# Layer 0: the tap path for three groups in four, indicator rows at image edges alone, the output's sum on GpSimd, and a new order of the work

## The reference

```
h  = w_hidden (384 x 64) * groupnorm(x) + b_hidden
h  = depthwise 3x3 convolution of h (w_dw, zero padding) + b_dw
q, k, v = h in three parts of 128 channels
out = irfft2(rfft2(q) * rfft2(k))      on patches of 8 x 8 pixels
out = layernorm of out over its 128 channels, times ln_w, plus ln_b
x   = x + w_proj (64 x 128) * (v * out) + b_proj
```

## Time and profile before

| | us |
|---|---|
| median of 3 runs | 8750.6 |
| lowest and highest | 8746.06 and 8751.87 |
| the profiled execution | 8754.59 |
| its span, first to last instruction | 8752.8 |

### The profile page before, as it was taken

How to read it: one execution, slowest core, us unless ns; L and a number is a source line. 1 busy time by engine, 2 the same in 40 slices (tenths; PEclk the granted TensorE clock), 3 DMA queues, 4 the chain that set the end, 5 groups by cost and what they waited for, 6 DMA issues and landing times. The chain is left out here.

```text
span 8752.8 us, 169999 instructions
## 1 busy us (share of the span) xinstructions
PE 8435.8 (96%) x57716; PEld 4818.6 (55%) x57716; DVE 7480.2 (85%) x9839; ACT 6324.6 (72%) x8629; POOL 4840.4 (55%) x2723
## 2 busy tenths in 40 slices
PE   2999999999999999999999999999879999999999
PEld 1666666666666666666666666666323333333333
DVE  6888888888888888888888888888759999999998
ACT  2777777777777777777777777777208888888887
POOL 1444444444444444444444444444109999999998
PEclk9999999999999999999999999999999999999999
DMA  6222222222222222222222212212694555555554
GB/s 154 54 68 61 55 68 63 55 67 54 64 68 53 64 56 66 64 56 65 64 49 55 54 43 54 54 43 54 146 203 114 119 119 119 119 119 119 119 119 111
DMA packets 613650, 711.27 MB, mean 81 GB/s; under 512 B 44029, under 2 KB 572507, under 8 KB 589575
## 3 DMA queue, kind: packets, MB, share of 16 engines
q1 hardware_dynamic: 611022, 690.44, 33.9%
q10 hardware_dynamic: 2488, 18.98, 1.0%
HBM read 548.96 MB, written 164.11 MB: 81 GB/s over the span
## 5 line engine op out<-in xcount | busy, mean ns | idle before, releaser
L625 PE MATMUL banks<-w_hi,hi_lo 128*128 128x256 f16 x18432 | 2362.6, 273 | 35.1 <-DVE hi_lo L927 35.1
L625 PEld LDWEIGHTS banks<-w_hi,hi_lo 128*128 128x128 f16 x18432 | 1737.7, 98 | 844.9 <-issue 533.5
L583 POOL TENSOR_TENSOR u_im<-q_im,k_swap 128x512 f32<-128x512 f32 x512 | 741.3, 1448 | 1810.4 <-ACT q_im L821 1723.8
L959 DVE SCALAR_TENSOR_TENSOR v_s<-banks,tap_w,v_s 128x512 f32<-128x512 f32 x2048 | 1535.1, 750 | 55.0 <-ACT v_s L810 0.6
L1511 PE MATMUL banks<-z,conv_w 128*128 128x512 f32 x3096 | 1556.0, 618 | 1.2 <-ACT z L1639 1.2
L1482 POOL TENSOR_TENSOR part_sum<-part_sum,prod 128x1024 f32<-128x1024 f32 x645 | 1525.2, 2365 | 52.2
L795 ACT ACTIVATE qk<-banks,inv_wscale 128x512 f32<-128x512 f32 x1024 | 706.5, 690 | 910.2 <-PE banks L625 903.7
L586 POOL TENSOR_TENSOR u<-u,u_im 128x512 f32<-128x512 f32 x512 | 725.3, 1417 | 766.8 <-DVE u L936 766.8
L625 PE MATMUL banks<-w_lo_pair,hi_pair 128*128 128x256 f16 x6144 | 1006.1, 273 | 0.0
L592 POOL TENSOR_TENSOR u<-u,u_mean 128x512 f32<-128x512 f32 x512 | 532.2, 1040 | 733.7 <-DVE u_mean L967 733.7
L1511 PEld LDWEIGHTS banks<-z,conv_w 128*128 128x128 f32 x3096 | 521.5, 188 | 628.1 <-issue 570.5
(11 more groups left out here) (252 smaller groups left out, 15777.1 us busy)
## 6 DMA issues: line engine op xcount, KB each, us to landing
xr<-in_x_dram SPq DMA_DIRECT2D x258, 640.0 KB, 9.1
xb<-y_scratch SPq DMA_DIRECT2D x262, 320.0 KB, 4.7
xa<-y_scratch SPq DMA_DIRECT2D x262, 256.0 KB, 5.4
x_res<-in_x_dram SPq DMA_DIRECT2D x258, 256.0 KB, 4.1
out_dram<-res SPq DMA_DIRECT2D x258, 256.0 KB, 3.3
y_scratch<-ys SPq DMA_DIRECT2D x256, 256.0 KB, 3.9
prod<-y_scratch SPq DMA_DIRECT2D x256, 256.0 KB, 5.6
xs<-in_x_dram SPq DMA_DIRECT2D x92, 512.0 KB, 7.4
```

The source lines that it names most:

```text
L583: nc.gpsimd.tensor_tensor(u_im[:], q_im[:], k_swap[:], ALU.mult).then_inc(u_made, 1)
L625: r = pe.matmul(out, px, w, start=n == 0, stop=n == 13)
L959: v.scalar_tensor_tensor(v_out, hidden_v[:, 1 + dc:GCOL + 1 + dc, 1 + dr:R + 1 + dr], tap_w[:, t:t + 1], v_out, ALU.mult, ALU.add).then_in ...
```

## The change

1. In each strip group 0 takes v from `conv_v`, groups 1, 2 and 3 from `hidden` and taps (before: 0 and 2, and 1 and 3). Every tap round is again one instruction on ScalarE and eight on VectorE.
2. The indicator rows L910 are written only where the strip's number is known when built and it, or the strip two before it, lies at an image's edge.
3. The sum `ys + t_n` is an instruction of GpSimd (`output_sum`), with new semaphores `t_made` and `fin_step`; VectorE keeps its statistics.
4. `means` becomes `sums` and `means`, `finish` becomes `scaled` and `shifted`, `imaginary` becomes `imaginary` and `complex_sum`, `root` and `freq_copy` are split likewise. All engines have a new order, written for one strip (`for h in range(2)`), and deeper: `body` is also issued for -1, 64 and 65, with filters `real...` for what does not exist. Every `forward` stands right behind another block and its wait is put ahead of that block's last matmul (`then_forward`). GpSimd does both halves of the low parts in a row. `hi_stacks` signals `tops_ready` of its own. The strip's statistics of x are read a body later.

The core of the diff (j = 4h, jp = 2h, js = h; lines marked with - are those of before, on the same engine):

```diff
# GpSimd
                 def body(i, first, stats, image, last):
-                    for k in range(8):
-                        if k % 4 == 2:
-                            pool.wait_ge(u_ready, i * 8 + (k - 1))
-                            low_parts(i * 2 + (k // 4 + 1), 0)
-                        if not (first and k == 0):
-                            imaginary(i, k, not (first and k == 1))
-                            less_mean(i, k)
-                        if k % 4 == 2:
-                            pool.wait_ge(u_ready, i * 8 + k)
-                            low_parts(i * 2 + (k // 4 + 1), 1)
+                        imaginary(i, j)
+                        complex_sum(i, j)
...
+                        low_parts(i, js + 1, 0)
+                        low_parts(i, js + 1, 1)
+                        less_mean(i, j)
+                        imaginary(i, j + 1)
+                        complex_sum(i, j + 1)
+                        less_mean(i, j + 1)
+                        imaginary(i, j + 2)
+                        complex_sum(i, j + 2)
+                        output_sum(i, jp - 1)
+                        less_mean(i, j + 2)
+                        imaginary(i, j + 3)
+                        complex_sum(i, j + 3)
+                        less_mean(i, j + 3)
+                        output_sum(i, jp)
+                def output_sum(i, jp):
+                    if real_pair(i, jp):
+                        out = ys[jp // 2 % 2][:, :, GCOL * (jp % 2):GCOL * (jp % 2) + GCOL]
+                        pool.wait_ge(fin_read, i * 4 + (jp + 1))
+                        pool.wait_ge(t_made, i * 4 + (jp + 1))
+                        nc.gpsimd.tensor_tensor(out, out, t_n[:].rearrange("p (c r) -> p r c", r=R), ALU.add).then_inc(fin_step, 1)
# TensorE
+                        inverse(i, j - 2)
+                        project(i, jp - 2, j - 1)
+                        value(i, j, image if h == 0 else None, then_forward=j)
+                        forward(i, j)
+                        hidden(i, j + 1, jp - 2)
+                        tile(i, j + 1, 0)
+                        tile(i, j + 1, 1)
+                        inverse(i, j - 1)
+                        tile(i, j + 1, 2)
+                        tile(i, j + 1, 3)
+                        variance(i, jp - 1)
+                        tile(i, j + 2, 0)
+                        project(i, jp - 1, j + 1, then_forward=j + 1)
+                        forward(i, j + 1)
+                        tile(i, j + 2, 1)
+                        hidden(i, j + 2, jp - 1)
+                        tile(i, j + 2, 2)
+                        inverse(i, j)
+                        tile(i, j + 2, 3)
+                        tile(i, j + 3, 0)
+                        tile(i, j + 3, 1, then_forward=j + 2)
+                        forward(i, j + 2)
+                        tile(i, j + 3, 2)
+                        tile(i, j + 3, 3)
+                        hidden(i, j + 3, jp - 1)
+                        inverse(i, j + 1)
+                        tile(i, j + 4, 0)
+                        tile(i, j + 4, 1)
+                        variance(i, jp, then_forward=j + 3)
+                        forward(i, j + 3)
+                        tile(i, j + 4, 2)
+                        tile(i, j + 4, 3)
# ScalarE
+                        qk_copy(i, j, 1)
+                        high_parts(i, js + 1)
...
+                        v_copy(i, j)
+                        first_tap(i, j + 1)
+                        query_imaginary(i, j)
+                        key_swap(i, j)
+                        square(i, j - 1)
+                        query_real(i, j)
+                        qk_copy(i, j + 1, 0)
+                        log_root(i, jp - 1)
+                        exp_root(i, jp - 1)
+                        qk_copy(i, j + 1, 1)
+                        query_imaginary(i, j + 1)
+                        qk_copy(i, j + 2, 0)
+                        first_tap(i, j + 2)
+                        query_real(i, j + 1)
+                        key_swap(i, j + 1)
+                        square(i, j)
...
# VectorE
+                        for row, col, edge in ((0, 4, 0), (R - 1, 5, S - 1)):
+                            if isinstance(s, int) and (s < 2 or s % S == edge or (s - 2) % S == edge):
+                                v.tensor_scalar(hi_ind[b][C:P, 1:W + 1, row], ind[C:P, :, row], par[b][C:P, col:col + 1], None, ALU.mult)
+                    if image is not None:
+                        x_chunk(i)
+                        next_means(image)
+                    for h in range(2):
+                        j, jp, js = 4 * h, 2 * h, h
+                        taps(i, j - 1, 2, 3)
+                        times_v(i, j - 3)
+                        taps(i, j - 1, 3, 4)
+                        sums(i, j - 2)
+                        taps(i, j - 1, 4, 5)
+                        means(i, j - 2)
+                        taps(i, j - 1, 5, 8)
+                        masks(i, js + 1)
+                        product(i, j - 1)
...
+                        shifted(i, jp - 2)
+                        scaled(i, jp - 2)
+                        output(i, jp - 3)
+                        if h == 0 and stats and not first and image is None:
+                            x_chunk(i)
+                        sums(i, j - 1)
...
+                        times_v(i, j - 2)
+                        means(i, j - 1)
+                        taps(i, j + 1, 0, 6)
+                        product(i, j)
+                        taps(i, j + 1, 6, 7)
+                        times_v(i, j - 1)
+                        taps(i, j + 1, 7, 8)
+                        output(i, jp - 2)
+                        sums(i, j)
+                        high_below(i, js + 1)
+                        means(i, j)
+                        scaled(i, jp - 1)
+                        high_stacks(i, js + 1)
+                        taps(i, j + 2, 0, 1)
+                        params(i, js + 2)
+                        taps(i, j + 2, 1, 3)
+                        product(i, j + 1)
+                        taps(i, j + 2, 3, 5)
+                        times_v(i, j)
+                        taps(i, j + 2, 5, 6)
+                        sums(i, j + 1)
+                        taps(i, j + 2, 6, 7)
+                        means(i, j + 1)
+                        taps(i, j + 2, 7, 8)
+                        both_stacks(i, js + 1)
+                        taps(i, j + 3, 0, 1)
+                        shifted(i, jp - 1)
+                        taps(i, j + 3, 1, 2)
+                        product(i, j + 2)
```

More of the change, by code:

```diff
@@ L527, in body @@
                     for b in range(2):
[L528 removed]
+                        if not last:
                             of, halves_before = i * 2 * R + (b + 2) * R, i * 4 + 2 * b + 2
@@ new lines, in inverse @@
+                def inverse(i, j, then_forward=None):
+                    if real(i, j):
+                        pe.wait_ge(u_ready, i * 8 + (j + 1))
+                        need(pe, w_ready, i * 8 + j)
+                        by_patch = b_o[:].rearrange("c (half t p x) -> c p t half x", half=2, t=2, p=2)
+                        for p in range(2):
+                            for t in range(2):
+                                block = slice(P * (2 * p + t), P * (2 * p + t) + P)
+                                if p and t and then_forward is not None:
+                                    transform_ready(i, then_forward)
+                                last = pe.matmul(by_patch[:, p, t], u[:, block], idft[:], start=True, stop=True)
+                        last.then_inc(inv_done, 1)
+                    elif then_forward is not None:
+                        transform_ready(i, then_forward)
@@ new lines, in variance @@
+                def variance(i, jp, then_forward=None):
+                    if real_pair(i, jp):
+                        pe.wait_ge(sq_ready, i * 8 + (2 * jp + 2))
+                        need(pe, fin_read, i * 4 + jp)
+                        for h in range(2):
+                            if h and then_forward is not None:
+                                transform_ready(i, then_forward)
+                            last = pe.matmul(b_var[C * h:C * h + C, :], mean_w[:, 0:C], sq[h][:], start=True, stop=True)
+                        last.then_inc(var_done, 1)
+                    elif then_forward is not None:
+                        transform_ready(i, then_forward)
@@ L761, in tail @@
-                def tail():
-                    transform_ready(NB, -1, True)
-                    forward()
-                    inverse(NB, -1, True)
-                    project(NB, 0)
-                    inverse(NB, 0, True)
-                    variance(NB, 1, True)
-                    project(NB, 2)
-                run(pe, body, tail)
+                    for h in range(2):
+                        j, jp, js = 4 * h, 2 * h, h
+                        inverse(i, j - 2)
```

(1 more changed line is left out.)

654 lines of the change are left out of this document (315 added, 339 removed).

## The result

The changed kernel takes 8945.5 us (median of 4 runs, 8943.4 to 8954.9) against 8748.3 of the kernel before (8745.6 to 8751.9): ratio 1.0226, interval [1.0214, 1.0239]. It is slower by 197 us; 8586 was predicted, and 8700 was the upper end. The profiled execution took 8943.63 us, with a span of 8941.8.

What follows compares the result with a forecast made beforehand. TensorE's instruction stream was taken as the bound, 46.8 us a strip. Strips of 45.3 give -192, x statistics +12, image edges +16: -164 from 8754.6, less 4 for the median, 8586 us; range 8410 to 8700.

Steps and rivals of the forecast that it cites:

- the chain by hand: Hand-traced sequence of one strip across the engines, with GpSimd holding VectorE: 45.3 us a strip in place of 46.8; chance 0.55.
- The first stack copy near 2.7 in place of 0.83: VectorE's first stack copy, held beside GpSimd's low part, was to take near 2.7 us in place of 0.83.
- Second low part 2.7: 22.3: GpSimd's second low part takes 2.7 us and ends 22.3 us after the strip's start in the hand-traced sequence.
- The sum of the output: Two sums a strip leave VectorE for GpSimd: 2 x 1.09 us and a wait, 2.4 us off VectorE.
- The indicator rows: Two rows leave VectorE in all but some 13 strips: 3.8 us, only 1.2 of them work.
- x statistics, +12: 46 bodies put 2.4 us of statistics ahead of VectorE's taps; 0.25 reaches the product, +12 us in all.
- SP: nothing: SP issues the same transfers; loads wait for a later output but have over half a strip until use: no cost.
- Clock: TensorE's clock was expected to fall only at the three image changes: 0, between -20 and +20 us.
- B: Rival: VectorE becomes the bound, stack and lower copies each held by GpSimd; 48.3 us a strip, 8970 us; chance 0.08.
- C: Rival: half of B's holds, strips of 46.5 to 46.9 us, no change, 8740 to 8790 us; chance 0.05 with D.
- D: Rival: indicator rows stay in every strip, 1.2 us more, 46.5 a strip, 8740 us; chance 0.05 with C.
- A: Rival: held time falls elsewhere or is hidden; TensorE stays the bound at 44.0 to 44.5 us, 8420 to 8484; chance 0.25.

Runs made afterwards that it cites:

- aftershift: The changed kernel with 40 useless TensorE products ahead of the first strip, outside every loop: 8779.9 us, ratio 1.0033 to the kernel before.
- order3: order2 with the four x statistics split two and two over a pair's strips and their load moved behind the loads of x on SyncE's queue: 8434.5 us.
- shortshift: The changed kernel with aftershift's 40 useless products and GpSimd's low parts cut from 128 to 16 columns: 8389.2 us, ratio 0.9587.
- meansact: The changed kernel with the scaling of the four means done by ScalarE in place of VectorE: 8887.6 us, ratio 1.0151 to the kernel before.
- meanshift: meansact with the 40 useless products of aftershift: 8729.5 us, ratio 0.9978 to the kernel before.
- sumback: The changed kernel with aftershift's 40 useless products and the sum of the output back on VectorE, gone from GpSimd: 8962.5 us, ratio 1.0236.
- indevery: The changed kernel with aftershift's 40 useless products and the two indicator rows multiplied in every strip again: 8842.2 us, ratio 1.0103.
- order2: order with the x statistics back where the change has them, and 40 useless products: 8502.0 us, ratio 0.9715 to the kernel before.
- order: The changed kernel with VectorE's below and stack copies moved ahead of taps, GpSimd's low parts later, x statistics at the strip's end: 9455.5 us, ratio 1.0799.

## Why the prediction was wrong

**The step that was absent: 165 us.** The prediction priced every instruction and none of the program's layout. Of the 360 us by which it was too low, 165 are instruction fetches in two loops with the lowered clock behind them (8945.5 against 8779.9). No row of before shows them: its loops lay where they don't fetch. The rule was in the Trainium skill, Runtime: NRT & Kernel Launch, Instruction fetch mechanics: instructions come in blocks of 16 KiB, and a taken branch to one outside the current window of two stalls the engine until it is fetched. The trace agrees on the blocks and on the stall, with 9 packets of 16384 bytes and waits of 1.7 and 2.65 us at the back edge. On the window it doesn't: loops of 1616 to 1672 instructions, over six blocks, turned back about a dozen times with 0 to 7 packets in all. The same section says that a long kernel needn't fit and that crossing a block is mostly hidden; in a loop the runs show otherwise, 22 to 84 us an image of some 12 turns.

**The term that was mis-sized: the strip, 47.0 for 45.3.** The other 194 us are this one. 8586 + 1.7 x 128 = 8804, and aftershift has 8780. Four things lie between: the x statistics and edge rows (+28 in my sum) cost nothing there (47.0 with statistics and without; 46.7 in the unrolled bodies at the edges, 7 us less in all); the image changes, "about 12 us each as before", took 7 to 8, together 13 us less; and the twelve strips of 48.7 cost 20 us more: 28 + 7 + 13 - 20 = 28, for the 24. In the chain by hand:
- TensorE's floor of 44.0 was right to a tenth (order3, shortshift). So were the taps at 0.75 us.
- VectorE's work at 39.0 a strip: order3, where little of VectorE's is held, has 333.65 / 374.4 x 44.0 = 39.2. Right.
- "The first stack copy near 2.7 in place of 0.83": the hold was real, but fell on the instruction ahead, the scaling of the means, left out as small. That is the step of the chain that failed. The wait fell on what VectorE was at when GpSimd started, whatever its size. meansact and meanshift show the price: 1.2 us in the strips without x statistics.
- "Second low part 2.7: 22.3": the two took 6.11, not 5.5, since the below copy ran in between at 2.02 for 0.9. Later holds (hi_ind, par, the lower copies) would be the other 0.5; no run has them alone.
- The sum of the output: 2.4 priced, 1.4 measured (sumback). The indicator rows: 1.2 priced, 0.5 measured (indevery). Both right in sign, both too high. VectorE's idle time (374.4 - 354.97 = 19.4 us in eight strips of the change) may swallow a part; no run shows it.
- x statistics, +12: nothing in aftershift, but 1.9 us a body in order2 and as much in meanshift. A term that is small while another wait hides it.
- "SP: nothing" was right for the change. order shows the price of the same question left unasked: 20 us in every second strip.
- Clock: I had it at the image changes alone (0, between -20 and +20). In the strips it cost about 53 of the 165 us, behind the stalls of the fetch, and 20 in aftershift, in the strips of 48.7. In the strips of 44.0 (order3, shortshift), where TensorE isn't idle, it stayed at 2.4 GHz.

**The rivals.** B had 8970, close to what was measured; that is chance, and B is refuted all the same: it asked for strips of 48.3, and they are 47.0. C (8740 to 8790, holds that eat the whole gain) is nearly what the change does once the fetch is away, 8780 with strips of 47.0; it had 0.05 together with D, because I took my own chain for more exact than a chain with four holds in it can be. A's 44.0 came in order3, once the low parts were moved away from the copies.

## What to carry to other kernels

Where GpSimd and VectorE hold each other, write down what each is at when the other starts: a 4-column instruction between two copies can carry the whole wait, and reordering can be worth more than removing work (order3 has all the work of the change and is 345 us faster than aftershift). When code is added to or taken from a program with loops, count the packets on the instruction queues inside the loops before believing any comparison; a few instructions ahead of the loops moved these kernels by 1 to 2%. When an instruction moves, look who queues behind its signal, the DMA queues first.

## What the runs showed of the hardware

- TensorE's loops of 1616 to 1672 instructions (101 to 105 KB) run with no instruction traffic or with 9 packets of 16384 bytes a turn, by their place alone; 12 instructions changed it for one loop. The price was 22 to 84 us an image, stalls and lowered clock together.
- TensorE's granted clock went to half for 3.4 or 6.8 us behind most stalls of the fetch in the change (126 us in two loops), and for 3.4 us in twelve strips of aftershift, behind a wait of 1.76 us that every strip has; never in the strips of 44.0 of order3 and shortshift, where TensorE isn't idle.
- A 128x4 multiplication on VectorE took 0.16 us, or 2.68 beside a GpSimd instruction; taps with an operand in PSUM stayed at 0.75 on average (0.73 to 0.75).
- VectorE and GpSimd together: three copies 2.18 us while GpSimd is idle, 3.60 beside its subtraction and its next product; GpSimd's 128x512 subtraction 1.04, or 2.08 and 2.42 beside VectorE's copies.
